# Graph network on one core: segment sums of the edge network with both tiles of a pair as fp32 matmuls

## The chip, the cores and the metric

One Trainium2 chip, of which the program uses one core. The time is the device time of one execution in microseconds (us). Three runs of the kernel before are given; another execution was taken with the hardware profiler, and the rows are of that one.

## What is computed

Four residual blocks on 3,125 nodes of 256 features: a graph network with an MLP on each edge, a mixture of experts, a two-layer neighbour average, a token-selecting feed-forward part. The change lies in the first. Cut to what matters:

```python
msg_input = jnp.concatenate([node_i, node_j, edge_features], axis=-1)   # 53125 edges
h = jax.nn.relu(msg_input @ mW1 + mb1)                                  # 512 hidden units
messages = h @ mW2 + mb2
aggregated = jax.ops.segment_sum(messages, i_idx, num_segments=N)
```

The kernel sums the hidden units `h` of each source node's edges first and multiplies by `mW2` later, for the sum is linear. With p = x @ mW1[node_i part] and q = x @ mW1[node_j part] computed ahead for each node, h of an edge is relu(p[i] + q[j] + edge_features @ mW1[last part] + mb1).

## The kernel before, in words

`stage_edge_network` (L536) works on edges that an earlier stage has put in order by blocks of 128 source nodes ("buckets"). A tile is 128 edges; two tiles of one bucket are a pair (a group of 256 slots). There are 232 pairs, and a loop over i of 29 trips takes eight pairs (G = 8, q = 0 to 7) each. The first and the last trip are written out, the 27 between are a hardware loop (`edges`, L587). Each engine runs its own `body`; nothing but semaphores sets the order between them.

For each pair, by engine:

- DVE, `one_hot` (L705): `hot`, for both tiles the 128 x 128 matrix that has a one where edge e has source node n. It is written for the pair after next.
- ACT, `widen` (L655): the edge's features doubled into `wide`, for the pair after next.
- TensorE, `transposes` (L765, L767), for the next pair: `wide` and `hot` of both tiles, four 128 x 128 transposes into `p_tr`. ACT, `take` (L660, L662), copies them to `trs` as fp32r.
- TensorE, `hidden` (L777, L780): for each tile three fp32r matmuls of 512 columns into `p_h`: the one-hot times the high and the low part of p, and the features times their weights.
- POOL gathers the 128 rows of q for each tile (L629), eight tiles ahead; each gather waits for the add that frees its buffer.
- DVE (L744): `p_h` plus the gathered rows gives `hb`, by tile.
- ACT (L680): relu, by tile. Tile 0 of a pair goes back into `hb` as fp32, tile 1 into `h_hi` as fp32r, that is, rounded to what an fp32r matmul reads.
- DVE, `low_part` (L720): relu(`hb`) - `h_hi` of tile 1 into `h_lo`, what the rounding lost.
- TensorE, `sums` (L783), for the pair before: tile 0 in one fp32 matmul (L790), tile 1 in two fp32r matmuls, by `h_hi` (L793) and by `h_lo` (L796); all three have 512 columns and add into `p_sum`. L785 waits until DVE has emptied that bank, L788 for the relu, L795 for the low part.
- DVE, `accumulate` (L713, L715): `p_sum` onto the bucket's row block of `C.agg`, and the degrees; for the pair two before.

So TensorE's order in a pair is `transposes(q+1)`, `hidden(q)`, `sums(q-1)`, and DVE's is `accumulate(q-2)`, `one_hot(q+2)`, `low_part(q-1)`, two adds of pair q.

In each trip both engines read the trip's bucket numbers into registers (`load_buckets`, L820): TensorE at q = 0, between `transposes` and `hidden` (L808); DVE at q = 0 behind the two adds (L749), and only then it runs `accumulate` of pair 6 of the trip before. L785 makes TensorE's `sums` of pair 0 wait for that one.

An fp32 matmul shows as two records of its line, each with a weight load; an fp32r one as one record.

Of the kernel before, what the change touches and what calls it, by code (L numbers as in the profile page):

```python
# [535 lines left out]
def stage_edge_network(nc, C, A, S):  # L536
# [7 lines left out]
    with ExitStack() as ctx:  # L544
# [7 lines left out]
        with ExitStack() as early:  # L552
            w_c = Mem(nc, early).sb("w_c", [P, HID])
            w_ch = Mem(nc, early).sb("w_ch", [P, HID])
        h_hi, h_lo = ([m.sb(f"h_{n}{b}", [P, HID], F32R) for b in range(2)] for n in ("hi", "lo"))
# [3 lines left out]
        hot = [m.sb(f"hot{b}", [P, 2, P], F32R) for b in range(4)]  # L559
# [13 lines left out]
        s_h, s_add, s_relu, s_low, s_sum, s_acc = (  # L573
            m.sem(n) for n in ("e_h", "e_add", "e_relu", "e_low", "e_sum", "e_acc"))
# [16 lines left out]
        with nc.Block() as block:  # L591
# [45 lines left out]
            def _(act):  # L637
# [27 lines left out]
                def body(i, first, last):  # L665
                    if first:
                        widen(i, 0)
                        widen(i, 1)
                        take(i, 0)
                    for q in range(G):  # L670
                        if not (last and q >= G - 2):
                            widen(*ahead(i, q, 2))
                        if not (last and q == G - 1):
                            take(*ahead(i, q, 1))
                        for j in range(2):
                            t = 2 * q + j
                            act.wait_ge(s_add, T * i + t + 1)

                            dst = hb[t % 4] if j == 0 else h_hi[q % 2]
                            act.activation(dst[:, :], hb[t % 4][:, :], ACT.Relu).then_inc(s_relu, 1)  # L680
# [4 lines left out]
            def _(dve):  # L685
# [31 lines left out]
                def low_part(i, q):  # L717

                    dve.wait_ge(s_relu, T * i + 2 * q + 2)
                    dve.scalar_tensor_tensor(out=h_lo[q % 2][:, :], in0=hb[(2 * q + 1) % 4][:, :], scalar=0.0,  # L720
                                             in1=h_hi[q % 2][:, :].bitcast(F32), op0=ALU.max,
                                             op1=ALU.subtract).then_inc(s_low, 1)

                def body(i, first, last):
# [6 lines left out]
                    for q in range(G):  # L731
# [6 lines left out]
                        if not (first and q == 0):  # L738
                            low_part(*behind(i, q, 1))
# [12 lines left out]
                    if last:  # L752
                        low_part(i, G - 1)
                        for q in (G - 2, G - 1):
                            accumulate(i, q, buckets.pop(0))
# [4 lines left out]
            def _(pe):  # L760
                def transposes(i, q):
# [4 lines left out]
                    for j in range(2):  # L766
                        last = pe.transpose(p_tr[q % 2][:, 2 + j, :], hot[q % 4][:, j, :].bitcast(F32), C.ident[:, :])  # L767
# [15 lines left out]
                def sums(i, q, first):  # L783
                    if not (first and q < 2):
                        pe.wait_ge(s_acc, 2 * (G * i + q) - 2)  # L785
                    for j in range(2):
                        t = 2 * q + j
                        pe.wait_ge(s_relu, T * i + t + 1)  # L788
                        if j == 0:
                            pe.matmul(p_sum[q % 2][:, :], hot[q % 4][:, j, :].bitcast(F32), hb[t % 4][:, :],  # L790
                                      start=True, stop=False)
                        else:
                            pe.matmul(p_sum[q % 2][:, :], hot[q % 4][:, j, :], h_hi[q % 2][:, :],  # L793
                                      start=False, stop=False)
                            pe.wait_ge(s_low, G * i + q + 1)  # L795
                            pe.matmul(p_sum[q % 2][:, :], hot[q % 4][:, j, :], h_lo[q % 2][:, :],  # L796
                                      start=False, stop=True).then_inc(s_sum, 1)
# [987 lines left out]
```

## Time and profile before

| | |
|---|---|
| median of 3 runs | 4267.46 us (4266.0 to 4267.86) |
| the profiled execution, its own time | 4262.32 us |
| its span, first to last instruction | 4260.5 us |
| mean granted TensorE clock over the span | 0.794 |
| edge network in the span | about 1068 to 2040 us |
| busy over the span: TensorE, its weight loads, DVE, ACT, POOL | 2569.0, 1655.4, 1849.4, 1032.5, 1935.2 us |

Times of rows are in us from the span's start, those marked ns in ns. Engines: PE is TensorE's matmuls, PEld its weight loads, DVE VectorE, ACT ScalarE, POOL GpSimd; PEldq is TensorE's instruction queue, whose register, semaphore and branch instructions don't count as busy. A row of a timeline gives start, duration, engine, line, operation, out<-in, how many instructions were merged (x2), and in brackets the idle time of the engine before it with what ended it. Matmuls are pipelined: a record lasts longer than the engine is taken by it, so distances between starts say what one costs. The granted clock is 1.00 at full speed (2.4 GHz) and 0.50 at half (1.2 GHz).

### The profile page before, as it was taken

What the parts mean: (1) busy time and instruction counts of PE and PEld (TensorE: products, weight loads), DVE (VectorE), ACT (ScalarE), POOL (GpSimd) and SP (SyncE); (2) the same over time, 40 slices, a digit from 0 to 9 for tenths busy, and PEclk for the clock granted to TensorE, in tenths of its full rate; (3) what the DMA queues carried; (4) which work ended last, traced back from release to release, by engine and by line L of the source; (5) the groups of instructions that cost most, each with busy time, mean ns of one, the idle gap of its engine ahead of it and who ended that gap; (6) DMA issues with size and microseconds to landing.
All of it is one profiled execution on the core that took longest, in us unless ns stands there. A gap on an engine that the chain in (4) does not pass through costs nothing. (4 is left out here: it accounts for less than half of the span.)

```text
span 4260.5 us, 47165 instructions
## 1 busy us (share of the span) xinstructions
PE 2569.0 (60%) x9048; PEld 1655.4 (39%) x9049; DVE 1849.4 (43%) x4308; ACT 1032.5 (24%) x2880; POOL 1935.2 (45%) x1900
## 2 busy tenths in 40 slices
PE   0121113866888888888797965555555555545398
PEld 0000001222555555555575643333333333333266
DVE  9500002556667766666222642222223322222479
ACT  0011112757545544444212220000000000000032
POOL 3877773000444444444111004666664566666520
PEclk9965556988899999999898987667666776766599
DMA  3111111113444444444532124333335333333521
GB/s 124 41 27 32 31 30 37 59 66 116 127 130 137 134 133 137 131 126 130 123 100 64 59 70 134 97 95 95 96 95 86 116 98 96 96 94 96 101 71 37
DMA packets 247793, 390.83 MB, mean 92 GB/s; under 512 B 82663, under 2 KB 169322, under 8 KB 246829
## 3 DMA queue, kind: packets, MB, share of 16 engines
q0 software_dynamic: 94976, 250.63, 21.5%
q1 hardware_dynamic: 129802, 110.65, 8.3%
q10 hardware_dynamic: 22948, 28.86, 2.2%
q8 instruction: 18, 0.29, 0.0%
q14 instruction: 49, 0.40, 0.0%
HBM read 308.20 MB, written 67.78 MB: 88 GB/s over the span
## 5 line engine op out<-in xcount | busy, mean ns | idle before, releaser
L1415 POOL DMA_INDIRECT nbr_yg<-y_d,nbr_idx x928 | 879.6, 948 | 457.5 <-issue 253.4
L1492 PE MATMUL nbr_sum<-nbr_yg,nbr_hot 128*128 128x258 f32 x1856 | 672.6, 512 | 640.2 <-issue 285.4
L1492 PEld LDWEIGHTS nbr_sum<-nbr_yg,nbr_hot 128*128 128x128 f32 x1856 | 439.4, 253 | 864.2 <-issue 544.0
L629 POOL DMA_INDIRECT qg<-q_d,rb x464 | 463.4, 999 | 529.7 <-DVE hb L744 445.8
L1454 DVE TENSOR_TENSOR nbr<-nbr_sum,nbr 128x258 f32 x464 | 197.5, 426 | 1018.5 <-remote 534.6
L299 POOL DMA_INDIRECT recs_d<-stage,stage_pos x416 | 454.0, 1091 | 177.5 <-issue 130.3
L492 PE MATMUL acc<-col_hot,lane_hot 128*128 128x464 f16 x832 | 244.9, 414 | 415.9 <-ACT lane_hot L325 277.4
L777 PE MATMUL p_h<-p_hl,trs 128*128 x928 | 338.6, 448 | 74.4 <-ACT trs L662 37.6
L325 ACT ACTIVATE lane_hot<-lane_one,val 128x128 f16<-128x128 f16 x832 | 255.8, 388 | 456.0 <-issue 327.7
L744 DVE TENSOR_TENSOR hb<-p_h,qg 128x512 f32<-128x512 f32 x464 | 301.2, 683 | 109.2 <-PE p_h L780 94.7
L457 DVE TENSOR_SCALAR lane_one<-iota_b,lane 128x128 f16<-128x128 f16 x416 | 107.0, 257 | 524.7 <-remote 338.7
L492 PEld LDWEIGHTS acc<-col_hot,lane_hot 128*128 128x128 f16 x832 | 63.5, 102 | 600.3 <-ACT lane_hot L325 410.6
L790 PE MATMUL p_sum<-hb,hot 128*128 128x512 f32 x464 | 254.4, 631 | 48.3 <-DVE deg_src L715 48.1
L680 ACT ACTIVATE hb<-hb 128x512 f32<-128x512 f32 x232 | 146.5, 632 | 373.2 <-DVE hb L744 330.0
L713 DVE TENSOR_TENSOR agg<-p_sum,agg 128x512 f32 x232 | 159.6, 688 | 169.4 <-issue 109.3
L777 PEld LDWEIGHTS p_h<-p_hl,trs 128*128 128x128 f32 x928 | 173.1, 207 | 107.3 <-issue 83.9
L780 PE MATMUL p_h<-w_cat,trs 128*128 128x512 f32 x464 | 197.7, 426 | 0.0
L793 PE MATMUL p_sum<-h_hi,hot 128*128 128x512 f32 x232 | 190.9, 823 | 0.0
L1435 ACT ACTIVATE z<-nbr_z 128x256 f32 x50 | 19.2, 385 | 695.5 <-remote 394.8
L1431 ACT ACTIVATE nbr_idx<-gidx 128x8 f32 (+1 forms) x116 | 23.8, 208 | 586.8 <-DMA nbr_yg<-y_d,nbr_idx 556.5
L720 DVE SCALAR_TENSOR_TENSOR h_lo<-hb,h_hi 128x512 fp32r<-128x512 f32 x232 | 158.7, 684 | 7.2 <-issue 4.0
L614 POOL MEMSET w_c<- 128x512 f32 x1 | 0.5, 525 | 352.7 <-POOLq L251 352.7
(257 smaller groups left out, 4054.9 us busy)
## 6 DMA issues: line engine op xcount, KB each, us to landing
nbr_yg<-y_d,nbr_idx POOLq DMA_INDIRECT x928
recs_d<-fill SPq DMA_DIRECT2D x16, 493.0 KB, 14.4
rb<-recs_d SPq DMA_DIRECT2D x58, 136.0 KB
qg<-q_d,rb POOLq DMA_INDIRECT x464
stage<-recs SPq DMA_DIRECT2D x52, 136.0 KB
recs_d<-stage,stage_pos POOLq DMA_INDIRECT x416
q_d<-q_out ACTq DMA_DIRECT2D x25, 256.0 KB
p_d<-p_out ACTq DMA_DIRECT2D x25, 256.0 KB
```

What stands on the lines that cost most here:

```text
L299: pool.indirect_dma_start(S.recs[:, :], bass.IndirectOffsetOnAxis(ap=stage_pos[b][:, j:j + 1], axis=0), stage[b][:, j, :], None).then_inc( ...
L325: act.activation(lane_hot[b][:, k, :], lane_one[b][:, :], ACT.Copy, scale=val[:, k, bass.ds(c, 1)]).then_inc(s_scaled, 1)
L492: last = pe.matmul(acc[k][:, 0:NCOL], lane_hot[b][:, k, :], col_hot[b][:, :], start=False, stop=False)
L629: pool.indirect_dma_start(qg[r][:, :], None, S.q[:, :], bass.IndirectOffsetOnAxis(ap=rb[b][:, r // 2, at:at + 1].bitcast(U32), axis=0)).th ...
L744: dve.tensor_tensor(hb[t % 4][:, :], p_h[t % 4][:, :], qg[t % TB][:, :], ALU.add).then_inc(s_add, 1)
L777: pe.matmul(p_h[t % 4][:, :], trs[q % 2][:, 2 + j, :], p_hl[:, bass.ds(bucket, 1), h, :].rearrange("p a n -> p (a n)"), start=(h == 0), st ...
L780: pe.matmul(p_h[t % 4][:, :], trs[q % 2][:, j, :], w_cat[:, :], start=False, stop=True).then_inc(s_h, 1)
L790: pe.matmul(p_sum[q % 2][:, :], hot[q % 4][:, j, :].bitcast(F32), hb[t % 4][:, :], start=True, stop=False)
L793: pe.matmul(p_sum[q % 2][:, :], hot[q % 4][:, j, :], h_hi[q % 2][:, :], start=False, stop=False)
L1415: pool.indirect_dma_start(yg[t][:, 0:D], None, S.y[:, :], bass.IndirectOffsetOnAxis(ap=idx[b][:, r:r + 1], axis=0)).then_inc(s_gath[t], 16)
L1454: dve.tensor_tensor(nbr, p_sum[q % SUMS][:, 0:W], nbr, ALU.add).then_inc(s_acc, 1)
L1492: last_mm = pe.matmul(p_sum[q % SUMS][:, 0:W], hot[t // HB_T][:, t % HB_T, :], yg[t][:, :], start=(j == 0), stop=(j == 1))
```

## The change

The odd tile's relu is written to `hb` as fp32, as the even tile's. `low_part`, its semaphore and the buffers `h_hi` and `h_lo` go. `sums` runs one fp32 matmul for each of the two tiles. `hot` is fp32 in name too (it was fp32r, and read as fp32 where that was wanted). `w_c` and `w_ch`, which had shared their SBUF with `h_hi` and `h_lo`, get their own.

```diff
--- before.py
+++ after.py
@@ -549,14 +549,11 @@
         assert NI * G == NG
         p_hl = m.sb("p_hl", [P, NT, 2, HID], F32R)
 
-        with ExitStack() as early:
-            w_c = Mem(nc, early).sb("w_c", [P, HID])
-            w_ch = Mem(nc, early).sb("w_ch", [P, HID])
-        h_hi, h_lo = ([m.sb(f"h_{n}{b}", [P, HID], F32R) for b in range(2)] for n in ("hi", "lo"))
+        w_c, w_ch = m.sb("w_c", [P, HID]), m.sb("w_ch", [P, HID])
         w_cat = m.sb("w_cat", [P, HID], F32R)
         rb = [m.sb(f"rb{b}", [P, GB, 2 * REC]) for b in range(2)]
         wide = [m.sb(f"wide{b}", [P, 2, P]) for b in range(2)]
-        hot = [m.sb(f"hot{b}", [P, 2, P], F32R) for b in range(4)]
+        hot = [m.sb(f"hot{b}", [P, 2, P]) for b in range(4)]
         trs = [m.sb(f"trs{b}", [P, 4, P], F32R) for b in range(2)]
         qg = [m.sb(f"qg{b}", [P, HID]) for b in range(TB)]
         hb = [m.sb(f"hb{b}", [P, HID]) for b in range(4)]
@@ -570,8 +567,8 @@
         s_gath = [m.sem(f"e_gath{b}") for b in range(TB)]
         s_init, s_agg_zero, s_prep = m.sem("e_init"), m.sem("e_agg_zero"), m.sem("e_prep")
         s_wide, s_hot, s_tr, s_trs = m.sem("e_wide"), m.sem("e_hot"), m.sem("e_tr"), m.sem("e_trs")
-        s_h, s_add, s_relu, s_low, s_sum, s_acc = (
-            m.sem(n) for n in ("e_h", "e_add", "e_relu", "e_low", "e_sum", "e_acc"))
+        s_h, s_add, s_relu, s_sum, s_acc = (
+            m.sem(n) for n in ("e_h", "e_add", "e_relu", "e_sum", "e_acc"))
         recs_v = S.recs[0:NSLOT, :].rearrange("(g p j) w -> p g (j w)", p=P, j=2)
 
         def ahead(i, q, n):
@@ -675,9 +672,7 @@
                         for j in range(2):
                             t = 2 * q + j
                             act.wait_ge(s_add, T * i + t + 1)
-
-                            dst = hb[t % 4] if j == 0 else h_hi[q % 2]
-                            act.activation(dst[:, :], hb[t % 4][:, :], ACT.Relu).then_inc(s_relu, 1)
+                            act.activation(hb[t % 4][:, :], hb[t % 4][:, :], ACT.Relu).then_inc(s_relu, 1)
 
                 edges(act, body)
 
@@ -713,13 +708,6 @@
                     dve.tensor_tensor(agg, p_sum[q % 2][:, :], agg, ALU.add).then_inc(s_acc, 1)
                     deg = C.deg_src[:, bass.ds(bucket, 1)]
                     dve.tensor_tensor(deg, deg_g[:, q:q + 1], deg, ALU.add).then_inc(s_acc, 1)
-
-                def low_part(i, q):
-
-                    dve.wait_ge(s_relu, T * i + 2 * q + 2)
-                    dve.scalar_tensor_tensor(out=h_lo[q % 2][:, :], in0=hb[(2 * q + 1) % 4][:, :], scalar=0.0,
-                                             in1=h_hi[q % 2][:, :].bitcast(F32), op0=ALU.max,
-                                             op1=ALU.subtract).then_inc(s_low, 1)
 
                 def body(i, first, last):
                     if first:
@@ -735,8 +723,6 @@
                             if not (first and q < 2):
                                 dve.wait_ge(s_sum, G * i + q - 1)
                             one_hot(*ahead(i, q, 2))
-                        if not (first and q == 0):
-                            low_part(*behind(i, q, 1))
                         for j in range(2):
                             t = 2 * q + j
                             dve.wait_ge(s_h, T * i + t + 1)
@@ -750,7 +736,6 @@
                             if not first:
                                 accumulate(i - 1, G - 2, buckets.pop(0))
                     if last:
-                        low_part(i, G - 1)
                         for q in (G - 2, G - 1):
                             accumulate(i, q, buckets.pop(0))
 
@@ -764,7 +749,7 @@
                     for j in range(2):
                         pe.transpose(p_tr[q % 2][:, j, :], wide[q % 2][:, j, :], C.ident[:, :])
                     for j in range(2):
-                        last = pe.transpose(p_tr[q % 2][:, 2 + j, :], hot[q % 4][:, j, :].bitcast(F32), C.ident[:, :])
+                        last = pe.transpose(p_tr[q % 2][:, 2 + j, :], hot[q % 4][:, j, :], C.ident[:, :])
                     last.then_inc(s_tr, 1)
 
                 def hidden(i, q, bucket, first):
@@ -786,15 +771,9 @@
                     for j in range(2):
                         t = 2 * q + j
                         pe.wait_ge(s_relu, T * i + t + 1)
-                        if j == 0:
-                            pe.matmul(p_sum[q % 2][:, :], hot[q % 4][:, j, :].bitcast(F32), hb[t % 4][:, :],
-                                      start=True, stop=False)
-                        else:
-                            pe.matmul(p_sum[q % 2][:, :], hot[q % 4][:, j, :], h_hi[q % 2][:, :],
-                                      start=False, stop=False)
-                            pe.wait_ge(s_low, G * i + q + 1)
-                            pe.matmul(p_sum[q % 2][:, :], hot[q % 4][:, j, :], h_lo[q % 2][:, :],
-                                      start=False, stop=True).then_inc(s_sum, 1)
+                        last = pe.matmul(p_sum[q % 2][:, :], hot[q % 4][:, j, :], hb[t % 4][:, :],
+                                         start=(j == 0), stop=(j == 1))
+                    last.then_inc(s_sum, 1)
 
                 def body(i, first, last):
                     if first:
```

## Rows read from the trace of the kernel before

**Rows 1.** Windows: length, busy PE, PEld, DVE, ACT, POOL (instructions), granted clock, DMA share, GB/s.
```profile
1341.09:1372.71 31.62, 26.39 (x112) 18.10 (x113) 23.13 (x48) 16.86 (x48) 15.62 (x16) 1.00 0.50 141
1406.65:1440.40 33.75, 29.22 (x113) 20.42 (x113) 23.63 (x48) 16.81 (x48) 16.81 (x16) 0.90 0.45 133
1068.00:2040.00 972.00, 830.32 (x3248) 567.12 (x3248) 677.83 (x1391) 488.36 (x1390) 455.76 (x456) 0.93 0.46 131
```

**Rows 2.** DVE's timeline, the add of pair 6 behind the bucket load, 27 trips apart.
```profile
1107.39 0.69 DVE L713 TENSOR_TENSOR agg<-p_sum,agg 128x512 f32 x1 [3.86 <-issue]
...
2015.28 0.69 DVE L713 TENSOR_TENSOR agg<-p_sum,agg 128x512 f32 x1 [4.61 <-issue]
```

**Rows 3.** TensorE's timeline of the full-clock trip: start, duration, line, [idle before].
```profile
1341.09 1.12 PE L790 MATMUL p_sum<-hb,hot 128*128 128x512 f32 x2 [2.31 <-DVE deg_src L715]
...
1345.04 1.02 PE L790 MATMUL p_sum<-hb,hot 128*128 128x512 f32 x2
...
1346.12 0.39 PE L796 MATMUL p_sum<-h_lo,hot 128*128 128x512 f32 x1
1346.35 0.38 PE L765 MATMUL p_tr<-ident,wide 128*128 128x128 f32 x2
...
1348.19 1.02 PE L790 MATMUL p_sum<-hb,hot 128*128 128x512 f32 x2
...
1358.17 1.02 PE L790 MATMUL p_sum<-hb,hot 128*128 128x512 f32 x2
...
1362.88 0.38 PE L767 MATMUL p_tr<-ident,hot 128*128 128x128 f32 x2
1365.60 0.73 PE L777 MATMUL p_h<-p_hl,trs 128*128 x2 [2.34 <-issue]
...
1372.71 0.69 PE L790 MATMUL p_sum<-hb,hot 128*128 128x512 f32 x1 [2.30 <-DVE deg_src L715]
```

**Rows 4.** DVE's timeline of the same trip, around the two holes.
```profile
1360.57 0.42 DVE L705 TENSOR_TENSOR hot<-iota_f,rb 128x256 fp32r<-128x256 f32 x1
1360.91 0.68 DVE L720 SCALAR_TENSOR_TENSOR h_lo<-hb,h_hi 128x512 fp32r<-128x512 f32 x1
...
1371.82 0.69 DVE L713 TENSOR_TENSOR agg<-p_sum,agg 128x512 f32 x1 [3.82 <-issue]
```

**Rows 5.** TensorE's queue (PEldq), lines 763 and 788, one trip: first and last start.
```profile
L763 PEldq EVENT_SEMAPHORE  x2: 51/51/51, 1428.7 to 1433.1; - x2
...
L788 PEldq ALU_OP  x2: 32/32/32, 1425.9 to 1426.4; - x2
```

**Rows 6.** TensorE's timeline of a trip with both falls of the clock.
```profile
1406.65 1.12 PE L790 MATMUL p_sum<-hb,hot 128*128 128x512 f32 x2 [1.95 <-DVE deg_src L715]
...
1408.41 0.68 PE L796 MATMUL p_sum<-h_lo,hot 128*128 128x512 f32 x1 [0.41 <-DVE h_lo L720]
...
1412.16 1.02 PE L790 MATMUL p_sum<-hb,hot 128*128 128x512 f32 x2
...
1427.95 1.02 PE L790 MATMUL p_sum<-hb,hot 128*128 128x512 f32 x2
...
1432.21 1.01 PE L777 MATMUL p_h<-p_hl,trs 128*128 x2 [2.34 <-issue]
...
1440.39 1.12 PE L790 MATMUL p_sum<-hb,hot 128*128 128x512 f32 x2 [1.78 <-DVE deg_src L715]
```

**Rows 7.** By windows and timeline: stretches behind three holes, and a hole of 1.68.
```profile
1408.60:1411.90 3.30, 3.30 (x11) 2.69 (x11) 3.20 (x7) 2.06 (x6) 1.86 (x2) 0.50 0.14 36
1244.40:1248.40 4.00, 4.00 (x21) 3.04 (x20) 4.00 (x9) 3.07 (x8) 2.21 (x3) 1.00 0.26 72
1432.60:1435.70 3.10, 3.10 (x9) 2.12 (x7) 1.38 (x2) 0.64 (x2) 0.44 (x1) 0.50 0.27 80
...
1242.25 1.12 PE L790 MATMUL p_sum<-hb,hot 128*128 128x512 f32 x2 [1.68 <-DVE deg_src L715]
...
1244.01 0.50 PE L796 MATMUL p_sum<-h_lo,hot 128*128 128x512 f32 x1 [0.42 <-DVE h_lo L720]
```

## The prediction

> **What bounds the kernel now.** Read the windows first [rows 1]. The edge network runs from about 1068 to 2040 us of the span; TensorE is busy 830 of these 972 us, DVE 678, ACT 488, POOL 456, at a mean clock of 0.93. The other stages are not touched. The stage is 29 trips of the loop over i, each of eight pairs. Two trips' lengths stand beside it in the rows: one wholly at full clock (1.00, that is 2.4 GHz) takes 31.62 us, one at 0.90 takes 33.75. So two things set the time of a trip, what TensorE must do and the clock that it is granted. The mean trip comes from two like events 27 trips apart [rows 2]: (2015.28 - 1107.39) / 27 = 33.63 us.
>
> Then TensorE's timeline of the full-clock trip [rows 3]. I name a moment by the start of the sums of pair q: S0 = 1341.09, S1 = 1345.04, S2 = 1348.19, S5 = 1358.17. A pair in the middle takes 3.15 us with no idle time: TensorE is the bound there, while DVE is busy 23.13 / 8 = 2.9 us a pair [rows 1]. The trip also has two holes. The first is before hidden() of the next trip's pair 0, at H = 1365.60, idle 2.34 us: TensorE's own queue loads eight bucket numbers (L808, L822). The second is before the next S0 = 1372.71, idle 2.30 us: `sums` waits in L785 for DVE, which loads its own bucket numbers for 3.82 us before it adds pair 6 [rows 4].
>
> So a trip is three stretches: S0 to S5, 17.08 us; S5 to H, 7.43; H to S0, 7.11. Together 31.62.
>
> **What the change adds.** The sums of a pair were one fp32 matmul of 512 columns (L790, two records) and two fp32r ones (L793, L796). From S1 to the L796 record are 1.08 us and from S1 to the transposes after it 1.31 us [rows 3]. The last fp32r matmul is thus 0.22 of this, and the fp32 one with L793 takes the 1.08, five times as long: an fp32 matmul costs four fp32r ones, 0.87 us. After the change a pair costs eight such passes, 1.75 us, in place of six: +0.44 us of TensorE a pair at full clock, twice that at half. The number of weight loads (two of each fp32 matmul, one of each fp32r) stays four a pair, and they are hidden behind the streams.
>
> The Trainium skill has another price. Perfetto Trace Analysis, section Engine Utilization, puts FP32_LOW_HIGH at half of the array's output rate, so two fp32r passes for an fp32 matmul and nothing added here. The rows speak against it, since 1.08 us hold one fp32 and one fp32r matmul. What the time would be by it is the last rival.
>
> **What it removes.** On DVE the 232 low parts, 0.68 us each [rows 4], of its 2.9 us a pair. DVE is not the bound in mid trip, so this buys no time there, but three waits go. (a) After the second hole, sums(0) waited for low(0): S0 to S1 took 3.95 us. It becomes one plain pair, 3.15 + 0.44 = 3.60 (rounded up). (b) The load of TensorE's bucket numbers starts earlier. Its queue runs ahead of the array: in another trip it had reached the waits of sums(6) (L788) at 1425.9 and 1426.4, while these matmuls ran at about 1428 [rows 5]. But L795 held it until low(6) was ready. In the full-clock trip low(6) ends at 1360.91 + 0.68 = 1361.59 and H follows 4.01 us later [rows 3, 4]. With L795 gone the queue is past the sums and the loop's branch earlier; what holds it is L763, the one-hot of the pair after next. That ends at 1360.57 + 0.42 = 1360.99, 2.82 after S5; sums(5) in front of it become 0.44 longer, so 3.26. From L763's record, 1428.7, to H of its trip, 1432.21, are 3.5 us of loads [rows 5, 6]. So S5 to H becomes 3.26 + 3.5 = 6.76, not 7.43. (c) DVE's stalls in mid trip no longer meet a queue of work behind them.
>
> ACT writes the odd tile's relu to `hb` in place of `h_hi`, same form and size: nothing. The wait for `hb` to be free lies behind `accumulate`, as now. No DMA, and nothing on SP's or POOL's queue, is moved; POOL's gathers wait for the adds and are busy 15.62 / 8 = 2.0 us a pair, within 3.60. The SBUF that `h_hi` and `h_lo` lay in costs nothing. What is late next in mid trip is again TensorE itself, 3.60 us against 2.2 of DVE.
>
> **The new trip at full clock.** S0 to S5: 5 x 3.60 = 18.00. S5 to H: 6.76. H to S0: 7.11, unchanged, for DVE's chain there (two adds, the load, the add of pair 6) starts at H; the longer sums(7) lie in the second hole, which shrinks from 2.30 to 1.86 us. Sum 31.87, against 31.62: the 3.5 us of added passes are given back but for 0.25. The first hole shrinks more. The transposes end at 1362.88 + 0.38, 5.09 after S5; that becomes 5.97 with two longer sums, and H comes at 6.76: 0.79 us idle in place of 2.34.
>
> **The clock.** It is here that I expect a gain, since the mean trip is 2.0 us over the one at full clock. What a fall costs now: after the first hole, H to S0 is 1432.21 to 1440.39, 8.18 us against 7.11, +1.07. After the second, S0 to S1 is 5.51 (1406.65 to 1412.16) against 3.95, +1.56 [rows 6]. With the change TensorE is the bound right behind the second hole, so there it would be half of the time spent low, for which I take 3.4 us (3.3 at 0.50 stand in one row [rows 7]), so 1.7. What a hole must be for a fall: 2.34 in front of 1432.21, then a stretch at 0.50. A hole of 1.95 and a 0.4 wait inside the sums behind it: 0.50. A hole of 1.68 with 0.42 behind it: still 1.00 [rows 6, 7]. After the change the first hole, 0.79, is far below all of these. The second is 1.86 with no wait behind it, less than 1.68 + 0.42. So I take falls as rare: 0.15 a trip. That is an inference from few sizes, and 1.86 lies near the edge; nor is a hole's length all that decides, since 2.34 in front of 1365.60 left that trip at 1.00 [rows 1, 3].
>
> **Sum.** 31.87 + 0.15 x 1.7 + 0.3 for DVE stalls that fall in the two gates (my choice: the mean trip has some 0.5 that clock falls don't explain, and mid-trip stalls are now covered) = 32.4, that is 1.2 less than 33.63. Over 27 trips -33 us. The first trip and the last have no such holes ahead and pay the passes: (8 + 7) x 0.44 less the shorter waits, +5. Net -28 us. The profiled execution took 4262.32 us around its span of 4260.5, and becomes 4234; the median of the runs shown, 4267.46, is 5.1 longer, and becomes 4239.5.
>
> Bounds: no fall and no stall, 31.87 a trip: -48 + 5 = -43, 4224. A fall at both holes in every trip: 31.87 + 0.3 + 1.7 + 1.07 = 34.94, +35 + 5 = +40, 4308.
>
> **Rivals.**
> 1. Falls in half of the trips, at the second hole: 33.0 a trip, -17 + 5 = -12, 4256. For: 1.86 is close to 1.95. Chance 0.20.
> 2. The other side: the clock still falls at the second hole in every trip. 31.87 + 0.3 + 1.7 = 33.87, +6 + 5 = +11, 4279. It decides from 0.75 falls a trip there. For: a hole of 1.95 was followed by one. Against: that had another 0.4 us wait behind it. Chance 0.17.
> 3. TensorE's queue cannot run so far ahead, and the loads start only when the transposes in front of them run, 5.35 after S5: S5 to H is then 8.85, a trip 34.3 at full clock and some 35.2 with a fall at the longer hole: +42 + 5, 4314. Against: the queue was 2 us ahead at L788. Chance 0.06.
> 4. The passes are simply paid, 8 x 0.44 = 3.5 us in each of 29 trips: +102, 4369. Against: sums(7) lie in front of a hole. Chance 0.03.
> 5. An fp32 matmul takes two passes, and none is added. 5 x 3.15 + 2.82 + 3.5 + 7.11 = 29.2, with 0.3 of stalls 4.1 less than now: -111, 4156. Against: the 1.08 us above. Chance 0.02. (This is the page's price.)
>
> That the change does something other than it says has no chance of note: the types of `hot` and `hb` settle which matmul is built.
>
> **The numbers.** The forecast case, 4240, has 0.52. The range takes it with its bound of 4224, rival 1 and rival 2, up to 4285. What a measurement of this kernel can tell from no change is 0.2%, 8.5 us. Faster by more: the forecast case, two thirds of rival 1, rival 5, rounded down for terms that I may have missed: 0.65. Within: the rest of rival 1 and some of rival 2: 0.15. Slower: 0.20.
>
> **What would show it.** Right: starts of L790 3.6 us apart in mid trip; no record of a low part; the idle before L777 at the trip's head 0.8 us; before the first L790 behind DVE's load 1.9; the stage's clock 0.97 or more in place of 0.93; the first adds behind DVE's load 32.4 us apart. Wrong: a 0.50 stretch behind most second holes (rivals 1, 2), an idle time of 2 us or more before L777 (rival 3), pairs 3.15 apart (rival 5).

## The result, and the profile after

4248.05 us median of 7 runs (4242.62 to 4253.53), against 4266.0 us for the kernel before in as many runs on the same chip (4262.25 to 4267.91): a ratio of 0.996, 95% interval 0.9949 to 0.9971. That is 18 us faster, where 28 were forecast (a median of 4240) and rival 1 gave 12 (4256). The profiled execution took 4242.62 us, its span 4240.8, against 4262.32 and 4260.5: 19.7 us less.

The windows of the kernel after: the stage, a trip without a fall of the clock, the one before it with a fall, and the stretch behind that one's hole (columns as in [rows 1]).

```profile
1068.00:2040.00 972.00, 868.71 (x3247) 543.20 (x3246) 544.90 (x1158) 503.89 (x1390) 437.69 (x458) 0.96 0.48 132
1141.22:1173.01 31.79, 28.89 (x113) 18.18 (x113) 18.69 (x40) 17.19 (x48) 15.51 (x16) 1.00 0.51 141
1107.88:1141.22 33.34, 30.52 (x112) 19.27 (x113) 18.87 (x40) 17.57 (x48) 15.17 (x16) 0.95 0.47 135
1109.10:1112.60 3.50, 3.50 (x10) 2.39 (x9) 2.25 (x6) 2.18 (x6) 1.89 (x2) 0.52 0.15 33
```

TensorE is 38 us busier in the stage than in [rows 1], DVE 133 us less, and the stage's granted clock is 0.96 in place of 0.93. DVE's timeline, the add of pair 6 behind the bucket load, 27 trips apart, answers to [rows 2]:

```profile
1106.99 0.69 DVE L708 TENSOR_TENSOR agg<-p_sum,agg 128x512 f32 x1 [3.86 <-issue]
...
1994.86 0.69 DVE L708 TENSOR_TENSOR agg<-p_sum,agg 128x512 f32 x1 [4.60 <-issue]
```

(1994.86 - 1106.99) / 27 = 32.88 us is the mean trip. It was 33.63, and 32.4 was forecast. TensorE's timeline of the trip without a fall, from S0 to the next S0, answers to [rows 3] (L774 is `sums`, L762 the first matmuls of `hidden`):

```profile
1141.22 1.98 PE L774 MATMUL p_sum<-hb,hot 128*128 128x512 f32 x4 [1.92 <-DVE deg_src L710]
...
1144.86 1.88 PE L774 MATMUL p_sum<-hb,hot 128*128 128x512 f32 x4
...
1148.40 1.88 PE L774 MATMUL p_sum<-hb,hot 128*128 128x512 f32 x4
...
1159.04 1.88 PE L774 MATMUL p_sum<-hb,hot 128*128 128x512 f32 x4
...
1165.88 0.72 PE L762 MATMUL p_h<-p_hl,trs 128*128 x2 [0.97 <-ACT trs L657]
...
1173.01 2.76 PE L774 MATMUL p_sum<-hb,hot 128*128 128x512 f32 x4 [1.92 <-DVE deg_src L710]
```

A pair takes 3.54 us (S1 to S2), S0 to S5 17.82, S5 to H 6.84, H to S0 7.13; the first hole is 0.97 us (0.9 in most trips), the second 1.92. The last row also shows what went otherwise than forecast: the first record behind the second hole lasts 2.76 us in place of 1.98, for the clock fell there (at 1174.1). In the trace it falls 17 times in the stage, where it had fallen 36 times: behind one first hole (of 2.06 us) and 16 of the 28 second ones. Before, it fell 20 times behind a first hole and 16 times behind a second one or the wait in the sums after it. So all of the falls that went were those of the first hole. That is the size of the gain: an estimate with the prediction's prices (1.07 us behind a first hole, 1.56 behind a second) gives 46 us for the 36 falls, and 17 falls at the 1.6 us measured below give 27, that is 19 us less, while the trip at full clock went from 31.62 to 31.79 us.

The idle time of TensorE by what ended it, in the stage; first the kernel after, then the one before:

```profile
PE p_sum L774 <- DVE deg_src L710: 53.9, 28, 2.6
PE p_h L762 <- ACT trs L659: 24.1, 21, 2.1
PE p_h L762 <- ACT trs L657: 3.8, 4, 1.0
PE p_h L762 <- issue: 3.3, 4, 0.9
```

```profile
PE p_sum L790 <- DVE deg_src L715: 48.1, 28, 2.3
PE p_h L777 <- ACT trs L662: 37.6, 18, 2.8
...
PE p_h L777 <- issue: 36.3, 16, 3.0
PE p_sum L796 <- DVE h_lo L720: 15.8, 34, 1.2
```

The first hole (the L762 and L777 rows) went from 73.9 to 31.2 us, the wait inside the sums from 15.8 to none, the second hole grew by 5.8. That is 52.7 us less of idle time against 38.4 more of work: 14 us less, of the stage's 16.6 (its matmuls ran from 1068.1 to 2038.4 us, now from 1067.6 to 2021.3).

### The profile page after: what moved, and what is told of

The parts are those of the page before. It is cut to its first block and busy times, and to the rows that moved or that the text cites. A ratio compares the mean times of both kernels' runs of the same rounds, so it can differ in the third digit from the quotient of the medians.

```text
span 4240.8 us, 46879 instructions
## 1 busy us (share of the span) xinstructions
PE 2606.2 (61%) x9048; PEld 1636.6 (39%) x9049; DVE 1718.6 (41%) x4076; ACT 1047.8 (25%) x2880; POOL 1910.2 (45%) x1900
## 5 line engine op out<-in xcount | busy, mean ns | idle before, releaser
L626 POOL DMA_INDIRECT qg<-q_d,rb x464 | 442.3, 953 | 531.3 <-DVE hb L730 429.9
L774 PE MATMUL p_sum<-hb,hot 128*128 128x512 f32 x928 | 456.2, 615 | 53.9 <-DVE deg_src L710 53.9
L675 ACT ACTIVATE hb<-hb 128x512 f32<-128x512 f32 x464 | 288.9, 631 | 315.8 <-DVE hb L730 298.1
L762 PE MATMUL p_h<-p_hl,trs 128*128 x928 | 316.9, 423 | 31.3 <-ACT trs L659 24.1
L774 PEld LDWEIGHTS p_sum<-hb,hot 128*128 128x128 f32 x928 | 176.0, 192 | 199.5 <-issue 177.8
L762 PEld LDWEIGHTS p_h<-p_hl,trs 128*128 128x128 f32 x928 | 162.8, 195 | 59.7 <-issue 38.7
L765 PE MATMUL p_h<-w_cat,trs 128*128 128x512 f32 x464 | 184.9, 398 | 0.0
L459 DVE TENSOR_SCALAR col_hot<-iota_h,col 128x464 f16<-128x464 int16 x416 | 143.6, 345 | 7.0 <-issue 7.0
```

The source lines that it names most:

```text
L626: pool.indirect_dma_start(qg[r][:, :], None, S.q[:, :], bass.IndirectOffsetOnAxis(ap=rb[b][:, r // 2, at:at + 1].bitcast(U32), axis=0)).th ...
L675: act.activation(hb[t % 4][:, :], hb[t % 4][:, :], ACT.Relu).then_inc(s_relu, 1)
L762: pe.matmul(p_h[t % 4][:, :], trs[q % 2][:, 2 + j, :], p_hl[:, bass.ds(bucket, 1), h, :].rearrange("p a n -> p (a n)"), start=(h == 0), st ...
L765: pe.matmul(p_h[t % 4][:, :], trs[q % 2][:, j, :], w_cat[:, :], start=False, stop=True).then_inc(s_h, 1)
L774: last = pe.matmul(p_sum[q % 2][:, :], hot[q % 4][:, j, :], hb[t % 4][:, :], start=(j == 0), stop=(j == 1))
```

## The experiments

Twelve kernels ran in three groups, each group on one chip and beside the kernel before. The chips differ. The kernel before took 3706 us on the first (chip S), 4268 on the second (chip L) and 4298 on the third (chip M); so kernels are compared by their ratios to it, or within a group. Stages that no kernel here touches make the difference; the last section comes back to it. TensorE's bucket load and DVE's are called the two loads.

| kernel | chip | us | ratio to before (95%) |
|---|---|---|---|
| low part as idle work (low_free) | S | 3709.8 | 1.0009 (0.9999 to 1.0018) |
| low part, and TensorE waits (low_wait) | S | 3777.1 | 1.0189 (1.0171 to 1.0206) |
| duplicate matmuls in the hole (dup_pair1) | S | 3685.1 | 0.9939 (0.9924 to 0.9955) |
| TensorE's load early (pe_swap) | S | 3656.0 | 0.9864 (0.9846 to 0.9882) |
| before again | L | 4269.3 | 1.0002 (0.9991 to 1.0013) |
| after again | L | 4247.4 | 0.9945 (0.9929 to 0.9961) |
| after, both loads early (both_early) | L | 4146.3 | 0.9707 (0.9692 to 0.9722) |
| before, both loads early | L | 4183.3 | 0.9795 (0.9778 to 0.9813) |
| after, third time | M | 4272.0 | 0.9943 (0.9930 to 0.9957) |
| before without its low part (no_low) | M | 4277.7 | 0.9958 (0.9943 to 0.9972) |
| both_early with the wait put back | M | 4213.4 | 0.9805 (0.9792 to 0.9818) |
| no_low, both loads early | M | 4173.0 | 0.9706 (0.9691 to 0.9722) |

**The low part: DVE's work or TensorE's wait?** Both kernels are the changed one with a low part that no matmul reads:

```diff
+                        if not (first and q == 0):
+                            low_part(*behind(i, q, 1))     # both kernels, DVE
...
+                        if j == 1:
+                            pe.wait_ge(s_low, G * i + q + 1)   # low_wait alone, before the odd tile's matmul
```

> The changed kernel with DVE's low part put back as work alone: 232 of them, 0.68 us each, into buffers that nobody reads; TensorE doesn't wait for them. Theory W (the low part cost time as a wait in TensorE's queue, not as work of DVE): DVE has 2.9 us a pair against 3.55 of TensorE, so the time is that of the changed kernel, 4248 within 6 us, and the idle time before L762-like matmuls at the head of a trip stays near 0.9 us. Rival D (DVE's work was what counted): back toward 4266 and over, for the passes stay: 4270 to 4290.

> As low_free, and TensorE waits for the low part of a pair before the odd tile's fp32 matmul, as the kernel before waited before its last fp32r matmul. Theory W: the queue is held until low(6) is done, some 3.8 us behind S5, and the loads of the bucket numbers end 4.0 us later: S5 to H 7.8 in place of 6.4, the first hole 2.0 us or more and the clock falling after some of them, a 0.4 us wait in sums(0). A trip gets 1.7 to 2.6 us longer: 4295 to 4320, slower than the kernel before by the passes that it pays. Rival D: equal to low_free, wherever that lies. If both are 4248, the gain came from neither.

Measured 3709.8 and 3777.1 us: the wait alone costs 67 us. TensorE's waits in the stage and what follows it (the 150.5 and 150.9 us stand ahead of its first pair), low_free first:

```profile
PE p_tr L761 <- DVE hot L701: 150.5, 1, 150.5
PE p_sum L785 <- DVE deg_src L711: 54.3, 28, 2.6
...
PE p_h L773 <- ACT trs L660: 25.4, 28, 1.7
```

```profile
PE p_tr L761 <- DVE hot L701: 150.9, 1, 150.9
PE p_h L773 <- issue: 54.4, 26, 2.1
PE p_sum L787 <- DVE deg_src L711: 31.0, 28, 2.6
PE p_sum L787 <- DVE h_lo L716: 21.5, 30, 0.7
PE p_h L773 <- ACT trs L660: 5.1, 3, 1.7
```

With the wait the first hole doubles, from 25 to about 60 us in all (0.9 to 2.1 us each), and it is "issue" that ends it: the bucket load, which starts later. Another 21.5 us are lost inside the sums, and the clock falls 31 times in place of 16. So (b) of the forecast holds: with the wait for `h_lo` in the queue the first hole is the long one, and with DVE's 0.68 us a pair alone, which low_free still has, it is not.

The total alone doesn't speak for theory W. By its ratio, 1.0009, low_free lies where rival D put it (4270 us of 4266), and theory W's 4248 would be 0.996. What speaks for W are the trips: their mean from the first second hole to the last is (1631.04 - 749.76) / 27 = 32.64 us with 16 falls, against 32.88 with 16 in the changed kernel of the result, so DVE's idle work lengthens none. The changed kernel itself did not run on chip S.

**Is it the length of the second hole that lets the clock fall?** The changed kernel with the first matmul of `hidden` run twice in pair 1, for both tiles; the duplicate is overwritten, and it lies ahead of the second hole:

```diff
+                        if q == 1:
+                            pe.matmul(p_h[t % 4][:, :], trs[q % 2][:, 2 + j, :], ..., start=True, stop=True)
                         for h in range(2):
                             pe.matmul(p_h[t % 4][:, :], trs[q % 2][:, 2 + j, :],
```

> The changed kernel with more work: in pair 1 of every trip, right ahead of the second hole, the first matmul of each tile (L762) runs twice; the second run overwrites the first. The results are the same. Adds two passes, 0.43 us, to each trip, inside the hole. Theory C (the clock falls after 16 of 28 second holes, since 1.91 us is just long enough): the hole becomes 1.45 us, falls behind it all but vanish, a trip takes 31.75 in place of 32.9: 4222, within 8 us. Rival (the falls have nothing to do with the length of this hole, or cost nothing): 4248 or up to 12 us more.

Measured 3685.1 us: 25 us faster than low_free with 0.43 us more work for TensorE in each trip. It also lacks low_free's idle work on DVE; but a trip without a fall takes 31.7 us in both, and the 15 falls that low_free has more, at 1.65 us each, are 25 us. TensorE's timeline, the first matmul behind four holes in a row; low_free, then dup_pair1:

```profile
1141.67 1.98 PE L785 MATMUL p_sum<-hb,hot 128*128 128x512 f32 x4 [1.92 <-DVE deg_src L711]
...
1173.37 3.08 PE L785 MATMUL p_sum<-hb,hot 128*128 128x512 f32 x4 [1.91 <-DVE deg_src L711]
...
1206.80 1.98 PE L785 MATMUL p_sum<-hb,hot 128*128 128x512 f32 x4 [1.93 <-DVE deg_src L711]
...
1238.48 3.33 PE L785 MATMUL p_sum<-hb,hot 128*128 128x512 f32 x4 [1.91 <-DVE deg_src L711]
```

```profile
1130.71 1.98 PE L778 MATMUL p_sum<-hb,hot 128*128 128x512 f32 x4 [1.44 <-DVE deg_src L710]
...
1162.44 1.98 PE L778 MATMUL p_sum<-hb,hot 128*128 128x512 f32 x4 [1.45 <-DVE deg_src L710]
...
1194.16 1.98 PE L778 MATMUL p_sum<-hb,hot 128*128 128x512 f32 x4 [1.44 <-DVE deg_src L710]
...
1225.84 1.98 PE L778 MATMUL p_sum<-hb,hot 128*128 128x512 f32 x4 [1.45 <-DVE deg_src L710]
```

With holes of 1.92 us every other one or so is followed by a stretch at half clock, and the trip takes 33.35 us in place of 31.7; with holes of 1.44 the trips take 31.7 us throughout, with one fall in the whole stage, behind its last hole, of 2.14. So the falls are what the changed kernel still loses.

But length alone doesn't decide: four holes equal to 0.02 us had two outcomes. The clock records of the traces show what sorts them. In each trace the stretches at half clock start only at moments of one even beat (to within 0.003 us), and what counts is where on that beat a hole ends. Of the holes of 1.90 to 1.95 us in low_free and the changed kernel, the 30 with a fall behind them end late between two such moments and the 23 without end early, and the two sets don't overlap. dup_pair1's 27 holes of 1.44 to 1.48 us are spread over the whole beat, 12 of them over the late part where each of the longer ones cost the clock, and none of them does. So the length counts too, and here that is shown.

**The holes taken away one by one.** First TensorE's load ahead of the transposes of pair 1:

```diff
                     for q in range(G):
+                        if q == 0:
+                            buckets = load_buckets(nc, pe, ...)
                         if not (last and q == G - 1):
                             transposes(*ahead(i, q, 1))
-                        if q == 0:
-                            buckets = load_buckets(nc, pe, ...)
```

> The changed kernel with TensorE's load of the bucket numbers ahead of the transposes of pair 1 in place of behind them, so that the one-hot which these wait for no longer holds the loads. Theory W (what holds the queue sets the first hole): the loads start at the relu of tile 13, 1.6 us behind S5, and end before sums(6) do; the first hole of 0.9 us is gone, a trip gets 0.9 shorter, the second hole stays 1.9: 4223, within 10 us. Rival (the loads don't start before the array comes to them): the hole grows by the transposes, which now lie behind it, no gain or some 10 us slower.

Measured 3656.0 us, 54 below low_free, so more than either figure expected. The first hole is gone: the load's 3.5 us now lie beside the sums of the pairs before. The second keeps its length, and yet the clock falls twice in the stage in place of 16 times. One of the 26 without a fall:

```profile
904.43 1.98 PE L774 MATMUL p_sum<-hb,hot 128*128 128x512 f32 x4 [1.91 <-DVE deg_src L710]
```

It would be natural to put this down to the first hole, 7 us earlier, that no longer stands there. The record doesn't bear that out. The 25 holes of 1.9 us without a fall end in the early part of the beat, where none of low_free or of the changed kernel cost the clock either, and the two with one end late; trips of 30.6 us, evenly spaced, happen to keep the holes at the harmless moments. So the 14 falls fewer, some 23 of the 54 us, are luck of the trip's length; the rest is the first hole's going. Next, DVE's load goes to the head of its trip as well, in the changed kernel (both_early) and in the kernel before; the two kernels themselves ran again beside them:

```diff
                     for q in range(G):
+                        if q == 0:
+                            buckets = list(load_buckets(nc, dve, ...))     # ahead of accumulate and one_hot
                         if q > 0 and not (first and q < 2):
                             accumulate(*behind(i, q, 2), buckets.pop(0))
```

> The kernel before, unchanged, for a profile on the chip of the other experiments, where it takes 3706 in place of 4266 us and the stages ahead of and behind the edge network are shorter. Theory S (part of the gain of the change was that DVE's stalls of about 1.7 us between instructions no longer reach TensorE, and this chip has none of them): trips 32.4 to 32.7 us here, in place of 33.6, with clock falls at both holes as there. Rival: the edge network is as there, 33.6 a trip, and the difference lies elsewhere.

> The changed kernel, unchanged, on this chip. Theory S: as low_free, which differs from it by idle work of DVE alone: 3709 within 5 us, no gain over the kernel before (3706), trips of 31.7 without and 33.35 with a clock fall, half of each. Rival (the gain doesn't depend on the chip): 18 us under the kernel before, 3688.

> The changed kernel with both loads of bucket numbers moved: TensorE's ahead of the transposes of pair 1, as in pe_swap, and DVE's from behind the two adds of pair 0 to the head of the trip, while DVE has 1.3 us to spare in each pair. Theory H (what is left over the passes are the two holes): the second hole shrinks from 1.9 to under 0.5 us, no clock falls, a trip is nearly eight plain pairs, 8 x 3.545 = 28.4, at most 29.3: 28 x 3.5 us less than the kernel after, 3595 to 3615. Rival (DVE's early load makes its adds of pair 0 late by as much): as pe_swap, 3656.

> The kernel before (three matmuls, low part, six passes a pair) with the same two moves. Theory H: with the holes gone the added passes of the change have nothing left to be paid from, and this one is the faster: eight pairs of 3.15 on TensorE, 25.2, but DVE has 8 x 2.9 + 3.8 = 27.0 us of work, and the loads of TensorE's queue are held by the low part. 27.2 to 28.5 a trip: 3570 to 3600, faster than both_early. Rival (the change gains in its own right): slower than both_early.

These texts reckon with chip S, but the four kernels ran on chip L, so theory S on the two chips wasn't tested. The kernel before measured 1.0002 of itself and the changed one 0.9945 of it, 21 us: the result stands. As ratios, both_early gains 2.9% and the kernel before with both moves 2.05%. I had expected the kernel before, with its fewer passes, to come out ahead once the holes were gone. It is 37 us behind. Windows of 200 us in mid stage, then TensorE's waits in them; both_early:

```profile
1300.00:1500.00 200.00, 196.00 (x767) 123.00 (x766) 127.67 (x275) 117.67 (x330) 103.76 (x110) 1.00 0.54 152
```

```profile
PE p_tr L750 <- DVE hot L700: 1.9, 2, 1.0
PE p_tr L750 <- issue: 1.8, 3, 0.9
```

and the kernel before with both moves:

```profile
1300.00:1500.00 200.00, 173.72 (x718) 120.35 (x716) 149.89 (x310) 109.71 (x312) 102.71 (x104) 0.96 0.51 145
```

```profile
PE p_tr L765 <- ACT wide L655: 9.1, 3, 3.1
PE p_tr L765 <- issue: 8.1, 3, 3.2
PE p_sum L796 <- DVE h_lo L720: 7.6, 8, 2.2
```

TensorE in both_early is busy 196 of 200 us at full clock, and the clock doesn't fall in the stage at all: there is next to nothing left to win by its waits. In the other a hole of 2.5 to 3.2 us stands before the transposes in nearly each trip (half of them put down to ACT's `widen`, half to "issue", the load), and low parts that come late stop the sums; the clock falls 20 times in its stage. That the holes and the stops come from L795 is my reading here; one of the next kernels puts that wait back.

**What do the passes cost?** Four kernels, all on chip M: the changed one again; the kernel before without its low part (five passes a pair in place of six, or of the changed kernel's eight; it leaves `h_lo` out of the sums); that one with both loads early; and both_early with low_wait's wait and idle work.

```diff
                             pe.matmul(p_sum[q % 2][:, :], hot[q % 4][:, j, :], h_hi[q % 2][:, :],
-                                      start=False, stop=False)
-                            pe.wait_ge(s_low, G * i + q + 1)
-                            pe.matmul(p_sum[q % 2][:, :], hot[q % 4][:, j, :], h_lo[q % 2][:, :],
                                       start=False, stop=True).then_inc(s_sum, 1)
```

> The changed kernel again, beside kernels that vary the wait and the passes. Two chips have been met: on one the kernel before takes about 4267 us, on the other 3706, with the two stages in front of the edge network shorter and the edge network about alike. On the first, the change is worth 18 to 21 us and I expect that again: 4247 us. On the second the nearest kernel to the change was the one with the low part kept as idle work: 3710 us, 0 to 0.2% over the kernel before. If idle work on DVE costs nothing there (theory W), the changed kernel takes the same 3710 there, its gain is gone on that chip, and the reason is to be read in the trips. If the idle work did cost something (rival D), it takes about 3690.

> The kernel before without the low part: the odd tile's sum is its high part's matmul alone, so five passes a pair in place of the changed kernel's eight, no work on DVE and no wait in TensorE's queue. It leaves the low part out of the sums, so its output is coarser. Theory L (a pass is paid only in the pairs before the queue's last gate; in the two pairs behind it the holes take it): three passes of 0.215 us less in five pairs, so 14.5 us from S0 to S5 in place of 17.7; the other two stretches stay within 0.5 us; the holes grow to about 1.6 and 2.55 us and the clock falls in nearly each trip, which gives 2 us back: a mean trip near 30, about 80 us under the changed kernel. Rival T (all passes are paid): 24 x 0.215 = 5.2 us a trip less, 27.7, about 145 us under it.

> The fastest kernel so far (the change, with both loads of bucket numbers moved early: 0.971 of the kernel before) with one thing put back: DVE works out a low part again, and TensorE waits for it ahead of the odd tile's fp32 matmul. The kernel before with both loads moved was 0.980, though its TensorE has 3.5 us less to do a trip; I hold the wait to be the reason. Theory W: the queue can't run ahead over the trip's border, idle times of 2 to 3 us before the transposes of pair 1 come back in most trips and 0.7 us of wait inside the sums, with falls of the clock behind them: 3 to 4 us in 28 trips, 85 to 110 us over the fastest kernel, so slower than the kernel before with both moves. Rival: the wait costs little once no load lies behind it, and it comes out within 20 us of the fastest kernel.

> The kernel before without its low part (five passes a pair, no wait, no DVE work for it) and with both loads moved early. It prices the passes where TensorE has no hole: the change with both loads moved kept TensorE busy 69 of 70 us at full clock. Theory P (a pass costs its 0.215 us where TensorE bounds, and no other engine is near: DVE 44, ACT 40, POOL 36 of 70 us busy): 24 passes a trip less, 5.2 us in 29 trips, 150 us under the change with both moves, a pair in mid trip 2.9 us. Rival Q (another engine's chain or the loads then set the pace): holes of 1 to 2 us a trip come back, and it gains only 60 to 110 us.

Both theories on no_low fell. With three passes fewer in every pair it takes 4277.7 us, 6 more than the changed kernel beside it; 80 and 145 less were expected. A pair in mid trip is indeed shorter (2.93 us). What it gives back is seen where DVE pauses. DVE's timeline of no_low, an add 1.93 us late, with nothing in the trace that it waited for; then TensorE's:

```profile
1464.65 0.68 DVE L735 TENSOR_TENSOR hb<-p_h,qg 128x512 f32<-128x512 f32 x1
1467.26 0.69 DVE L735 TENSOR_TENSOR hb<-p_h,qg 128x512 f32<-128x512 f32 x1 [1.93 <-remote]
...
1470.34 0.42 DVE L705 TENSOR_TENSOR hot<-iota_f,rb 128x256 fp32r<-128x256 f32 x1
```

```profile
1470.91 0.41 PE L755 MATMUL p_tr<-ident,wide 128*128 128x128 f32 x2 [1.66 <-DVE hot L705]
```

The one-hot behind the late add is late too, and TensorE stands for it. The waits in the stage of no_low, TensorE's and DVE's (36.6 us of the first row stand ahead of the first pair):

```profile
PE p_tr L755 <- DVE hot L705: 104.5, 44, 36.6
PE p_h L767 <- ACT trs L662: 66.8, 27, 2.8
PE p_sum L780 <- DVE deg_src L715: 48.3, 28, 2.6
```

```profile
DVE hb L735 <- remote: 71.8, 36, 4.0
```

In the changed kernel on the same chip TensorE waits 37.4 us for one-hots, nearly all ahead of the first pair, and 35.0 on the L659 copies. So 67 us more go on late one-hots, and 32 on a longer first hole, which the added passes had filled. The clock takes its part as well: it falls 28 times in place of 15, and 13 of the low stretches are twice as long as the usual one, where the changed kernel has one such. My reading is that the pauses of DVE, which a backlog of eight passes covers, reach TensorE where it has five; it is not shown by itself, for DVE's "remote" waits are also fewer in the changed kernel there, 38.4 us against 77.1. In the window from 1068 to 2045 us TensorE is busy 767.5 us in no_low and 867.8 in the changed kernel, at clocks of 0.92 and 0.96: 100 us of work gone, and the stage no shorter (965 us against 959).

With both loads early it is the same: five passes 0.9706 of the kernel before, eight 0.9707 (150 us apart by theory P). Its row beside both_early's:

```profile
1300.00:1500.00 200.00, 171.28 (x696) 114.65 (x695) 123.85 (x269) 112.92 (x324) 101.58 (x107) 0.95 0.53 149
```

TensorE has 25 us less to do in 200 us, and the other engines get as far as they did. And with the wait put back, eight passes take 0.9805 and the kernel before's six 0.9795, again alike. The wait costs 1% there, 42 us: half of what I expected, though with 2.2 us holes in every trip, as the waits of that kernel in the same window show:

```profile
PE p_tr L761 <- issue: 13.2, 6, 2.2
```

The clock fell behind only three of these holes in the whole stage: trips of 30.8 us kept the others early on the beat, as in pe_swap, so the 42 us hold few falls and another trip length could make the wait dearer.

The four with both loads early, on two chips: eight passes without the wait 0.9707, with it 0.9805; five without it 0.9706, six with it 0.9795. The wait is worth 1%, two or three passes nothing that shows. The two with a wait ran on different chips and have it at different places, so only the pair without one is a clean comparison of passes. One pair of kernels speaks otherwise: low_wait, with eight passes and a wait, is 1.9% over the kernel before, with six and a wait, on chip S. Its wait stands ahead of four passes, the kernel before's ahead of one, so this is no clean price of the passes; it suggests that they aren't free where the wait stays.

## Why the prediction was right, and where its sum was off

The verdict (faster, by less than 1%) and the way to it held, but for the number of clock falls. 4248 lies between the forecast case (4240) and rival 1 (4256), and of the signs one of those for "wrong" came: a stretch at half clock behind most second holes, 16 of 28. The stage's clock was 0.96, where 0.97 or more was a sign of "right". Step by step:

- **A pair, 3.60 us forecast:** 3.54. Two more passes cost 0.39 us, not 0.44; no_low gives the same from below, (3.54 - 2.93) / 3 = 0.20 a pass. The rival of two passes for an fp32 matmul is out: pairs would have stayed 3.15 apart. It was the prediction's reading of the Trainium skill's Perfetto Trace Analysis, section Engine Utilization, which halves the array's output rate for FP32_LOW_HIGH but doesn't say that an fp32 matmul runs as that. Another page of the Trainium skill, FP8 and Floating Point Precision, section TensorE Precision Notes, says that true fp32 takes four passes through the array; the trace agrees, with 0.20 us for each of them.
- **S0 to S5, 18.00:** 17.82. **S5 to H, 6.76:** 6.84. **H to S0, 7.11:** 7.13. Together 31.79 for 31.87. That the queue runs ahead once L795 is gone, and that the first hole then shrinks to 0.79 (0.9 measured), is what low_free against low_wait confirmed, 67 us apart. Rivals 3 and 4 are out by the same rows.
- **Falls of the clock, "I take falls as rare: 0.15 a trip":** this step failed. It is 0.57 to 0.6 (16 in 28 second holes), which is rival 1. The argument was that a hole of 1.86 us with no wait behind it is milder than one of 1.68 followed by 0.42. The hole came out at 1.92, and at that length the moment of the hole decides, which the prediction didn't reckon with; so that it was 16 and not 2 or 28 is in part luck of the trip's length. The price of a fall, 1.7 us, was right: trips of 33.35 against 31.75, 1.6. So the falls take 16 x 1.6 / 27 = 0.95 us from the mean trip where 0.26 were allowed. The text itself had said that the inference stood on few sizes and that 1.86 lies near the edge.
- **DVE's stalls, 0.3 a trip:** what is left, 32.88 - 31.75 - 0.95 = 0.2.
- **The ends:** the 27 trips account for 907.89 - 887.87 = 20.0 us, the first and last trip give back 3.4 (the stage is 16.6 shorter) where 5 were taken, and the stages around differ by 3.1: 20.0 - 3.4 + 3.1 = 19.7 us.

A reason that the prediction gave for its gain was too simple. It read the passes as paid in mid trip and given back at the holes (5 x 0.44 us in S0 to S5 against two shorter stretches). Within a trip that is so. But against a kernel that has neither the added passes nor the wait the eight passes cost nothing in all, on chip M: late one-hots, the longer first hole and the clock take what fewer passes save. So the gain is the wait's going, by way of the first hole and the clock falls behind it, and the price of it was near nil.

One thing stays open. On chip S the changed kernel itself was not run, and its nearest kin, low_free, is level with the kernel before there (1.0009). In the trace of low_free no wait of DVE in the stage is put down to "remote", in no_low's 71.8 us are, on chip M. It would fit that on a chip without such pauses the kernel before has less to lose by its wait, and the change then gains nothing; trips there could also just fall otherwise on the clock's beat. Neither was shown: the kernel before has no profile from chip S.

## What to carry to other kernels

A wait in an engine's queue costs what is queued behind it, not what it waits for: an address or register load behind it can no longer run ahead. Work can be traded for the removal of such a wait, even where the engine that takes the work looks like the bound, but price the trade against idle stretches and clock falls as well as in mid loop. And when the idle stretches come from register loads, moving the loads in the queue can be worth more than the arithmetic: both moves with the change gave 4146.3 us, 0.9707 of the kernel before (0.9692 to 0.9722), some six times the change's own gain (122 us against 21 on that chip). Of the kernels here only the one that leaves the low part out reaches as low a ratio (0.9706).

## What was not expected of the hardware

With 0.43 us of useless matmuls added to each trip the kernel was 25 us faster than low_free, because the hole behind them was 1.44 us and not 1.92, and TensorE then stayed at 2.4 GHz.

Holes of one length had different outcomes by their moment alone. Those of 1.9 us were followed by 1.2 GHz in 15 of 27 cases in low_free and in 2 of 27 in pe_swap, and all 54 sort without an exception by where they end on the even beat at which the clock falls. So two kernels with the same holes can differ by 14 falls, some 23 us, through the length of their trips.

Chips differ by 560 to 590 us on the same program. The windows from the start to the edge network's first pair, first on the result's chip (kernel after), then on chip S (low_free), whose code is the same there:

```profile
0.00:1068.00 1068.00, 352.78 (x1096) 116.14 (x1098) 409.22 (x1189) 309.03 (x913) 487.67 (x443) 0.74 0.17 56
```

```profile
0.00:709.00 709.00, 311.50 (x1094) 113.39 (x1095) 410.51 (x1186) 299.06 (x913) 476.55 (x443) 0.84 0.26 85
```

DVE has the same work, 409 and 411 us, in 1068 and in 709 us. On the slower chip its largest wait is this one, in pieces of up to 27 us, and it isn't among the large ones on chip S:

```profile
DVE lane_one L457 <- remote: 386.8, 59, 27.0
```

What "remote" stands for was not tried. The pauses of 2 us that reached TensorE in no_low bear the same name.
